# Turning the probabilities as float32r, one block later, after a move inside SBUF: a perceiver block on one core

## The chip, the core and the metric

The kernel runs on one core of one Trainium2 chip. The metric is device time in microseconds (us) of one execution; lower is better. A core has TensorE (PE in the profile, with its weight loads as PEld), VectorE (DVE), ScalarE (ACT), GpSimd (POOL), and SyncE (SP), which here only issues DMAs.

## What is computed

64 tokens `x` of width 512 attend to a context of 6272 rows, then pass a quantised linear block and a second one with a Fourier update. Nearly all the time is the first part, cut here to what matters:

```python
q = (layernorm(x) @ Wq + bq).reshape(64, 8, 4, 128)     # 8 key heads, 4 query heads each
k, v = split(ctx @ Wkv + bkv)                           # 6272 x 8 x 128 each
attn = softmax(einsum(q, k) / sqrt(128))                # per head: 256 query rows x 6272 keys
x = x + einsum(attn, v) @ Wo + bo
x = x + attention_block(layernorm(x), NF4[codes] * scales, lora_a, lora_b)
x = x + base_and_fourier_update(layernorm(x))
```

The 4-bit codes of the second part are expanded to float32 weights, a tile of 128 x 512 at a time.

## The kernel before, in words

The context is walked in 7 chunks of 896 rows (`NCH`, 7 tiles of 128), and in each chunk over the 8 key heads (`NKV`). One head of one chunk is a *block*: 56 blocks, i = 0 to 55 (`NB`). A float32 product is made of three float32r products of rounded parts (`split_matmuls`, L71 to 75): hi x hi, lo x hi, hi x lo. ScalarE rounds a result from PSUM to its hi part, VectorE subtracts to get the lo part.

TensorE's order in block i is written out by hand (`block_work`, L836): the scores of the block (12 products of 448 columns, two halves of the keys for two halves of the 256 query rows), the previous block's weighed values (`prev_values`, 21 products of 256 columns), in even blocks the values of *two* heads for all 7 tiles (`values`, 84 products of 256 columns, into the two banks of `p_kv` in turn), the first half of the next block's keys (`project_keys`, 12 products of 448 columns), then the turns of this block's probabilities in four groups (`turn_probs`, L678 to 691: 4, 4, 4 and 2 transposes of 128 x 128 float32, `probs` as weights, `ident` moving), with the turn of the previous output (`turn_output`) and the second half of the keys between them. Long blocks (even) and short ones (odd) so alternate.

VectorE takes the scores out of PSUM with their minimum (L1314), makes the change of the row maximum (`drop`), splits turned tiles (`pt_lo`, L1291), values (L1279) and keys (L1281), adds the output (`acc`, L1302), and between them merges the lines of one weight tile (L1326, L1330). ScalarE makes the exponentials in place in `probs` (L1171), rounds (L1092, L1103) and draws four of a tile's eight lines (L1127). GpSimd draws the other four (L534), casts codes (L530), joins and scales the tile (L554, L563), and splits context pieces (L522). SP's queue is in order: an issue that waits holds all behind it. It brings the codes (`codes_of`), the scales, the context pieces (`load_ctx`, through one buffer `ctx_st`), and writes each expanded tile to memory (`tile_out`, L400). In the first chunk it also brings the query weights (`load_wq`) and key and value weights (`load_wkv`), and TensorE makes the eight query products (L700) between the other work. In the last chunk freed space takes the weights of what follows, and in the last block the attention output is projected between the last turns (L775).

The two lines that the change centres on:

```python
pe.wait_ge(exp_ready, 2 * i + 2)
m = nc.tensor.transpose(p_t[:, c % 2, col:col + P], probs[:, r, t * P:(t + 1) * P], ident[:])
```

Of the kernel before, what the change touches and what calls it, by code (L numbers as in the profile page):

```python
# [17 lines left out]
P = 128  # L18
# [47 lines left out]
PAIR_PIECES = (5, 5, 5, 1)  # L66
# [62 lines left out]
def whole(nc, ctx_t, x, wq, bq, wkv, bk, bv, codes, scales, weights, wo, bo, lora_a, lora_a_down, lora_b, lora_b_down,  # L129
# [4 lines left out]
    with ExitStack() as st:  # L134
# [8 lines left out]
        pt_hi = sb(st, "pt_hi", [P, CT, ROWS], F32R)  # L143
        pt_lo = sb(st, "pt_lo", [P, CT, ROWS], F32R)
# [8 lines left out]
        slots = sb(st, "slots", [P, 7, TW], F32)  # L153
# [18 lines left out]
        pool_passed = sem("pool_passed")  # L172

        NB = NCH * NKV
        KV_USES = CT + 4

        ACT_LINES = ((1, 1), (2, 2), (4, 4), (5, 5))

        def v_use(s, h, t):
            return 2 + KV_USES * (4 * s + h // 2) + t

        def k_use(s, h, c):

            return 2 + KV_USES * (4 * s + h // 2) + CT + 2 * (h % 2) + c

        def v_bank(h, t):
            return (h // 2 + t) % 2

        def k_bank(h, c):
            return (h // 2 + 1 + c) % 2
# [116 lines left out]

        def tile_of(n, j):  # L310
            return tile_quarters(n)[:, 2 * j:2 * j + 2]
# [53 lines left out]
        def _(sp):  # L365
# [35 lines left out]

            def ring_slots(h):

                first, end = AHEAD[h]
                freed = (end - 1 - RING_ODD) // 4
                if freed < 0:
                    sp.wait_ge(kv_psum, k_use(NCH - 2, NKV - 2, 1) + 1)
                else:
                    sp.wait_ge(kv_psum, k_use(NCH - 1, 2 * freed, 1) + 1)
                for n in range(first, end):  # L410
                    load_slot(n)
# [26 lines left out]
            def chunk(s, last):  # L438
                piece = 0
                for pair in range(NKV // 2):  # L440
# [3 lines left out]
                    def load(q):  # L444
                        if not last and q < PAIR_PIECES[pair]:
                            load_ctx(s + 1, piece + q, start and q == 0)
# [4 lines left out]
                    load(0)  # L451
                    codes_of(n + 2)
                    if start:
                        load_wq(4)
                    load(1)
                    if start:
                        load_wq(5)
                        load_wkv(4)
                        load_wkv(5)
                    tile_out(n)  # L460
                    scales_of(n + 1)
                    if start:
                        load_wq(6)
# [5 lines left out]
                    if start:  # L469
                        load_wq(7)  # L470
                    load(2)
                    load(3)
                    if not end:
                        codes_of(n + 3)
                    if start:
                        load_wkv(6)
                        load_wkv(7)
# [18 lines left out]
                    piece += PAIR_PIECES[pair]  # L496
# [19 lines left out]
        def _(pool):  # L516
# [20 lines left out]
            def first_lines(n, first=False):  # L537
# [4 lines left out]
                line(6, 6)  # L542
# [49 lines left out]
            for dst, src in ((bq_sb, bq), (bk_sb, bk), (bv_sb, bv)):  # L592
                pool.dma_start(dst[:], src).then_inc(vecs_in, 16)
            narrow(0, True)
            first_lines(0, True)

            def chunk(s, par, last):
                piece = 0
                for pair in range(NKV // 2):
                    n = NKV * s + 2 * pair  # L600

                    def split(q):
                        if not last and q < PAIR_PIECES[pair]:
                            split_ctx(s + 1, piece + q, 1 - par)

                    if s == 0 and pair == 1:
# [6 lines left out]
                    last_line(n)  # L613
                    narrow(n + 1)
                    split(0)
                    add_rowsum(n, 2 * pair)
                    join(n)
                    first_lines(n + 1)
                    split(1)
                    split(2)  # L620
                    last_line(n + 1)
# [3 lines left out]
                    if end:  # L625
                        wait_apart(pool, kv_psum, k_use(NCH - 1, NKV - 2, 1) + 1, pool_passed)
# [6 lines left out]
                    join(n + 1)  # L633
                    first_lines(n + 2)
                    split(4)
                    piece += PAIR_PIECES[pair]

# [8 lines left out]
            last_line(NB)  # L646
# [7 lines left out]
            last_line(NB + 1)  # L654
# [3 lines left out]
        def _(pe):  # L658
            def project_keys(bank, half, h, c, k):
# [3 lines left out]
                m = split_matmuls(nc, p_kv[:, bank, 0:HALF], wkv_hi[:, k, cols], wkv_lo[:, k, cols],  # L663
# [5 lines left out]
            def static_first(i):  # L669
                return isinstance(i, int) and i == 0  # L670

            def turn_output(i):

                pe.wait_ge(o_out, i + 1)
                if not static_first(i):
                    pe.wait_ge(ot_added, i)
# [4 lines left out]
            def turn_probs(i, c, skip):  # L681

                if c == 0:
                    pe.wait_ge(exp_ready, 2 * i + 2)
                if not skip:
                    pe.wait_ge(pt_split, 4 * i + c - 1)
                for t in range(2 * c, min(2 * c + 2, CT)):
                    for r in range(RT):
                        col = (t % 2) * ROWS + r * P
                        m = nc.tensor.transpose(p_t[:, c % 2, col:col + P], probs[:, r, t * P:(t + 1) * P], ident[:])  # L690
                m.then_inc(pt_psum, 1)

            def query_product(h):

                pe.wait_ge(wq_in[h % 2], 16 * (h // 2 + 1))
                if h >= 1:
                    pe.wait_ge(q_out, h)
                for k in range(KT):
                    for i in range(2):
                        m = nc.tensor.matmul(p_o[HALVES[i], 0:TW // 2], xt[:, k], wq_sb[h % 2][:, k, HALF_COLS[i]],  # L700
# [12 lines left out]
            def scores(i, h, kuse, static):  # L713
                if i < NKV:
                    pe.wait_ge(q_split, h + 1)
                for c in range(2):
                    pe.wait_ge(kv_split, kuse + c + 1)
                    for r in range(RT):
                        bank = p_s[:, r, 0:HALF] if c == 0 else p_kv[:, k_bank((h - 1) % NKV, r), 0:HALF]
                        if c == 0 and not static:  # L720
                            pe.wait_ge(scores_out, 4 * i - 3 + r)
                        m = split_matmuls(nc, bank, q_hi[:, h, r * P:(r + 1) * P],
# [4 lines left out]
            def values(s, h, half, queries={}):  # L727
                if s == 0:
                    pe.wait_ge(wkv_split, wkv_turn(h + 1) + 1)
                for t in range(CT):  # L730
                    for work, head in queries.get(t, ()):
                        work(head)
                    if t < 2:
                        pe.wait_ge(scores_out, 4 * (NKV * s + h) + 4)
                    pe.wait_ge(kv_split, v_use(s, h, t) - 1)
                    cols = slice((NKV + h) * D, (NKV + h + 2) * D)
                    for k in range(KT):
                        keys = slice(t * P, (t + 1) * P)
                        m = split_matmuls(nc, p_kv[:, v_bank(h, t), 0:2 * D], ctx_hi[half][:, k, keys],
                                          ctx_lo[half][:, k, keys], wkv_hi[:, k, cols], wkv_lo[:, k, cols],  # L740
                                          start=(k == 0), stop=(k == KT - 1))
                    m.then_inc(kv_psum, 1)

            def prev_values(s, h):

                i = NKV * s + h - 1
                hp = (h - 1) % NKV
                pair = 4 * s + h // 2 - (1 if h % 2 == 0 else 0)
                pe.wait_ge(pt_split, 4 * i + 4)
                pe.wait_ge(kv_split, 2 + KV_USES * pair + CT)  # L750
# [978 lines left out]
```

## Time and profile before

| | us |
|---|---|
| median of 3 runs | 1031.01 |
| lowest, highest | 1030.47, 1032.99 |
| span of the profiled execution, first to last instruction | 1028.8 |

The profiled execution is one more execution, and its own time beside its span isn't listed apart from the three runs. Busy times are shares of the span. TensorE's records overlap, as a product is started before the last has drained, so the pace is read from start to start and not from a record's length.

### The profile page before, as it was taken

The numbers are of one execution on the slowest core, as the hardware profiler recorded it, in microseconds if no ns is written. First come the engines' busy times: TensorE is split into PE (matmuls) and PEld (weight loads), VectorE is DVE, ScalarE is ACT, GpSimd is POOL, SyncE is SP. The second block draws the span as 40 slices with busy tenths as digits, with TensorE's granted clock in tenths as the row PEclk, the third lists the DMA queues.
The fourth block names the chain that finished last, engine by engine and source line by source line (L and its number), as shares of the span: only waits on it lengthen the run. The fifth ranks groups of instructions, "written<-read, shape, count | busy, mean of one in ns | idle before, by whom it ended". The sixth has DMA issues, their size and how long they took to land.

```text
span 1028.8 us, 19701 instructions
## 1 busy us (share of the span) xinstructions
PE 1015.2 (99%) x7083; PEld 934.4 (91%) x7083; DVE 752.1 (73%) x1680; ACT 590.3 (57%) x1254; POOL 482.4 (47%) x640
## 2 busy tenths in 40 slices
PE   8999999999999999999999999999999999999998
PEld 6889999999999999999999999999999999999744
DVE  5777778766877677767776687767776687767766
ACT  6456666555665567555665566555665566565431
POOL 2344554455444555445544555545545534544341
PEclk9999999999999999999999999999999999999999
DMA  9832211122212222122211222221222213552895
GB/s 321 263 107 59 65 56 58 58 70 76 60 51 65 65 60 70 42 70 70 70 58 50 71 61 65 64 57 59 68 55 68 72 42 122 168 153 84 250 351 175
DMA packets 74097, 99.01 MB, mean 96 GB/s; under 512 B 8752, under 2 KB 43072, under 8 KB 74000
## 3 DMA queue, kind: packets, MB, share of 16 engines
q1 hardware_dynamic: 72384, 95.95, 30.9%
q10 hardware_dynamic: 1424, 1.51, 0.4%
q8 instruction: 57, 0.93, 0.4%
q0 software_dynamic: 192, 0.29, 0.1%
q14 instruction: 40, 0.33, 0.1%
HBM read 82.91 MB, written 14.81 MB: 95 GB/s over the span
## 4 chain that ended last, share of the span: by engine, by line
PE 93%; DVE 4%; ACT 1%; DMA 1%; issue 1%; ACTq 0%; POOL 0%; DVEq 0%; POOLq 0%
PE p_kv L73 20%; PE p_kv L74 20%; PE p_kv L75 20%; PE p_t L690 8%; PE p_o L73 4%; PE p_o L74 4%; PE p_o L75 4%; PE p_s L73 2%; PE p_s L74 2%; PE p_s L75 2%; PE p_s L775 2%; PE p_o L700 1%; PE p_ot L678 1%; DVE slots L1326 1%; DVE probs L1314 1%; DMA ctx_st<-in_ctx_t 1%
## 5 line engine op out<-in xcount | busy, mean ns | idle before, releaser
L534 POOL TENSOR_SCALAR slots<-code 128x512 f32<-128x512 bf16 x232 | 154.4, 665 | 223.3 <-DVE slots L1330 150.3
L1326 DVE TENSOR_TENSOR slots<-slots 128x512 f32<-128x512 f32 x232 | 167.7, 723 | 1.9
L1279 DVE TENSOR_TENSOR v_lo<-p_kv,v_hi 128x256 fp32r<-128x256 f32 x196 | 83.2, 424 | 113.2 <-ACT v_hi L1092 113.2
L1127 ACT ACTIVATE slots<-code,drop_and_offsets 128x512 f32<-128x512 bf16 x232 | 148.5, 715 | 28.4 <-POOL slots L554 24.9
L554 POOL TENSOR_TENSOR slots<-slots 128x512 f32<-128x512 f32 x58 | 74.8, 1290 | 185.8 <-DVE slots L1326 185.8
L1092 ACT ACTIVATE v_hi<-p_kv 128x256 fp32r<-128x256 f32 x196 | 75.2, 384 | 146.5 <-PE p_kv L75 146.1
L1281 DVE SCALAR_TENSOR_TENSOR k_lo<-p_kv,bk_sb,k_hi 128x448 fp32r<-128x448 f32 x112 | 76.3, 682 | 104.1 <-ACT k_hi L1092 103.3
L1291 DVE TENSOR_TENSOR pt_lo<-p_t,pt_hi 128x512 fp32r<-128x512 f32 x224 | 133.5, 617 | 23.7 <-ACT pt_hi L1103 23.6
L1092 ACT ACTIVATE k_hi<-p_kv,bk_sb 128x448 fp32r<-128x448 f32 x112 | 70.8, 633 | 132.0 <-PE p_kv L75 131.0
L1103 ACT ACTIVATE pt_hi<-p_t 128x512 fp32r<-128x512 f32 x224 | 114.9, 541 | 40.4 <-PE p_t L690 40.4
L73 PE MATMUL p_kv<-wkv_hi,ctx_even_hi 128*128 128x256 f32 x448 | 126.4, 282 | 0.2 <-issue 0.2
L75 PE MATMUL p_kv<-wkv_hi,ctx_even_lo 128*128 128x256 f32 x448 | 125.9, 281 | 0.0
L74 PE MATMUL p_kv<-wkv_lo,ctx_even_hi 128*128 128x256 f32 x448 | 125.8, 281 | 0.0
L1171 ACT ACTIVATE probs<-probs,mins 128x896 f32<-128x896 f32 x112 | 115.5, 1033 | 0.0
L690 PE MATMUL p_t<-ident,probs 128*128 128x128 f32 x784 | 113.1, 272 | 0.2 <-ACT probs L1171 0.2
L73 PE MATMUL p_o<-pt_hi,v_hi 128*128 128x256 f32 x392 | 111.0, 283 | 0.0
L74 PE MATMUL p_o<-pt_lo,v_hi 128*128 128x256 f32 x392 | 110.9, 283 | 0.0
L75 PE MATMUL p_o<-pt_hi,v_lo 128*128 128x256 f32 x392 | 110.8, 283 | 0.0
L690 PEld LDWEIGHTS p_t<-ident,probs 128*128 128x128 f32 x784 | 95.4, 140 | 15.0 <-issue 0.8
L73 PE MATMUL p_kv<-ctx_even_hi,wkv_hi 128*128 128x448 f32 x256 | 99.2, 388 | 0.6 <-issue 0.5
L74 PE MATMUL p_kv<-wkv_lo,ctx_odd_hi 128*128 128x256 f32 x336 | 95.1, 283 | 0.0
L75 PE MATMUL p_kv<-wkv_hi,ctx_odd_lo 128*128 128x256 f32 x336 | 94.9, 282 | 0.0
(239 smaller groups left out, 2705.0 us busy)
## 6 DMA issues: line engine op xcount, KB each, us to landing
code<-in_codes SPq DMA_DIRECT2D x58, 256.0 KB, 2.7
scale<-in_scales SPq DMA_DIRECT2D x114, 128.0 KB, 3.1
expanded_weights<-slots SPq DMA_DIRECT2D x56, 256.0 KB, 2.1
ctx_st<-in_ctx_t SPq DMA_DIRECT2D x96, 112.0 KB, 2.0
ring_hi<-expanded_weights SPq DMA_DIRECT2D x22, 256.0 KB, 6.0
ring_lo<-expanded_weights SPq DMA_DIRECT2D x22, 256.0 KB, 6.1
wq_hi<-in_wq SPq DMA_DIRECT2D x4, 1024.0 KB, 7.5
wq_lo<-in_wq SPq DMA_DIRECT2D x4, 1024.0 KB, 7.3
```

Of the source, the lines that this page charges most:

```text
L73: nc.tensor.matmul(out, hi, rhi, start=start, stop=False)
L74: nc.tensor.matmul(out, hi, rlo, start=False, stop=False)
L75: return nc.tensor.matmul(out, lo, rhi, start=False, stop=stop)
L534: nc.gpsimd.tensor_scalar(slots[:, slot, :], code16[:], LINES[j][0], LINES[j][1], ALU.mult, ALU.add).then_inc(pool_lines, 1)
L690: m = nc.tensor.transpose(p_t[:, c % 2, col:col + P], probs[:, r, t * P:(t + 1) * P], ident[:])
L1092: nc.scalar.activation(dst, src, ACT.Identity, bias=0.0 if bias is None else bias).then_inc(kv_rounded, 1)
L1103: nc.scalar.activation(pt_hi[:, 2 * c:2 * c + n, :].rearrange("p t q -> p (t q)"), p_t[:, c % 2, 0:n * ROWS], ACT.Copy).then_inc(pt_rounde ...
L1127: nc.scalar.activation(slots[:, slot, :], code16[:], ACT.Identity, bias=offsets[:, k:k + 1], scale=LINES[j][0]).then_inc(act_lines, 1)
L1171: nc.scalar.activation(probs[:, r, :], probs[:, r, :], ACT.Exp, bias=mins[:, h, r, now:now + 1], scale=-1.0, accum_out=rowsum[:, par, r:r ...
L1279: nc.vector.tensor_tensor(dst, src, hi.bitcast(F32), ALU.subtract).then_inc(kv_split, 1)
L1291: nc.vector.tensor_tensor(pt_lo[:, 2 * c:2 * c + n, :].rearrange("p t q -> p (t q)"), p_t[:, c % 2, 0:n * ROWS], pt_hi[:, 2 * c:2 * c + n, ...
L1326: nc.vector.tensor_tensor(slots[:, slot, :], slots[:, slot, :], slots[:, other, :], ALU.max).then_inc(merged, 1)
```

## The change

- `turn_probs` for block i - 1 now stands in block i, behind that block's scores. SP first copies the two halves of `probs` inside SBUF into a second tile `probs_r`, bit for bit, and the turn reads that as float32r with an identity of float32r. The last block alone (i = 55) is still turned in float32 from `probs`.
- VectorE waits for the copy before it writes the next scores; SP waits for the earlier turns (`pt_psum`) and each half's exponentials.
- The values of two heads are made over two blocks: 4 tiles in the even one, 3 in the odd one. The first and the last pair make all 7 in the even one.
- The turned tiles have a ring of 4 places instead of 7, and the weighing is done in two parts (tiles 0 to 3, tiles 4 to 6). The space pays for `probs_r`, as does one line slot less.
- The first half of the next keys goes to `p_s` instead of `p_kv`, the orders of ScalarE, VectorE and GpSimd follow, with GpSimd's line 6 drawn only after the second merge, into a slot that this has freed. Context pieces are spread anew (5 a pair of blocks).

Cut to its core:

```diff
+        PT_TILES = 4
+        probs_r = sb(st, "probs_r", [P, RT, CHUNK], F32R)
+        ident_r = sb(st, "ident_r", [P, P], F32R)
-        ACT_LINES = ((1, 1), (2, 2), (4, 4), (5, 5))
+        ACT_LINES = ((2, 2), (5, 5), (1, 1), (4, 4))
+        SPLIT_TILE = 4
+        def value_tiles(i):
+            if i in (0, NB - 2):
+                return range(CT)
+            if i in (1, NB - 1):
+                return range(0)
+            return range(SPLIT_TILE) if i % 2 == 0 else range(SPLIT_TILE, CT)
+        def k_place(h, c):
+            return p_s[:, 0, 0:HALF] if c == 0 else p_kv[:, h % 2, 0:HALF]
...
+            def move_probs(i):
+                if i > 0:
+                    sp.wait_ge(pt_psum, 4 * i)
+                for r in range(RT):
+                    sp.wait_ge(exp_ready, 2 * i + 1 + r)
+                    sp.dma_start(probs_r[:, r].bitcast(F32), probs[:, r]).then_inc(probs_moved, 16)
...
                     load(0)
+                    move_probs(n)
                     codes_of(n + 2)
                     load(1)
+                    load(2)
                     tile_out(n)
                     scales_of(n + 1)
+                    load(3)
...
+                        move_probs(n + 1)
                         codes_of(n + 3)
...
-            def last_line(n):
-                wait_apart(pool, merged, 6 * n + 1, pool_passed)
+            def last_lines(n):
+                wait_apart(pool, merged, 6 * n + 2, pool_passed)
                 line(7, 1)
+                line(6, 3)
...
-                if c == 0:
-                    pe.wait_ge(exp_ready, 2 * i + 2)
+                if i < NB - 1:
+                    pe.wait_ge(probs_moved, 32 * (i + 1))
+                        if i < NB - 1:
+                            m = nc.tensor.transpose(p_t[:, c % 2, col:col + P].bitcast(F32R), probs_r[:, r, keys], ident_r[:])
...
+            def block_work(s, h, half):
+                scores(i, h)
+                turn_probs(i - 1, 0)
+                turn_probs(i - 1, 1)
+                next_keys(i, h, half, 0)
+                weigh_values(i - 1, 0, SPLIT_TILE)
+                turn_probs(i - 1, 2)
+                turn_probs(i - 1, 3)
+                if i > 2:
+                    turn_output(i - 2)
+                for t in value_tiles(i)[:SPLIT_TILE]:
+                    value_tile(i, h, half, t)
+                next_keys(i, h, half, 1)
+                weigh_values(i - 1, SPLIT_TILE, CT)
...
+            (ScalarE)
+                output_out(i - 2); round_probs(i - 1, 0); round_probs(i - 1, 1)
+                weigh(i, h, half, 0); weigh(i, h, half, 1)
+                round_keys(i, h, 0)
+                round_probs(i - 1, 2); round_probs(i - 1, 3)
+                (value tiles, with lines and a context piece between); round_keys(i, h, 1)
...
+            (VectorE)
+                if i > 0:
+                    dve.wait_ge(probs_moved, 32 * i)
+                score_stats(i, h, half)
+                split_probs(i - 1, 0); split_probs(i - 1, 1)
+                merge(i, 0); merge(i, 1)
+                split_keys(i, h, 0)
+                merge(i, 2)
+                split_probs(i - 1, 2); split_probs(i - 1, 3)
+                add_output(i - 2, (h - 2) % NKV)
+                (three times: split_values, merge); split_keys(i, h, 1)
```

The lines for ScalarE and VectorE are gathered from their `block_work`, several to a line.

## Rows read from the trace of the kernel before

**Rows 1.** The page's head: busy us (share of the span) and instructions of each engine.
```profile
PE 1015.2 (99%) x7083; PEld 934.4 (91%) x7083; DVE 752.1 (73%) x1680; ACT 590.3 (57%) x1254; POOL 482.4 (47%) x640
```

**Rows 2.** The chain that ended last, shares of the span by engine and by line.
```profile
PE 93%; DVE 4%; ACT 1%; DMA 1%; issue 1%; ACTq 0%; POOL 0%; DVEq 0%; POOLq 0%
PE p_kv L73 20%; PE p_kv L74 20%; PE p_kv L75 20%; PE p_t L690 8%; PE p_o L73 4%; PE p_o L74 4%; PE p_o L75 4%; PE p_s L73 2%; PE p_s L74 2%; PE p_s L75 2%; PE p_s L775 2%; PE p_o L700 1%; PE p_ot L678 1%; DVE slots L1326 1%; DVE probs L1314 1%; DMA ctx_st<-in_ctx_t 1%
```

**Rows 3.** Stretches: length, each engine's busy us (instructions), clock, DMA share, GB/s.
```profile
0.00:48.00 48.00, 43.46 (x276) 34.16 (x277) 29.17 (x65) 24.42 (x45) 13.34 (x28) 1.00 0.89 292
48.00:157.40 109.40, 106.99 (x739) 99.06 (x738) 81.76 (x182) 66.15 (x140) 54.73 (x70) 1.00 0.27 82
157.40:922.30 764.90, 764.88 (x5291) 730.66 (x5290) 566.70 (x1268) 457.33 (x982) 378.72 (x498) 1.00 0.24 69
```

**Rows 4.** The chain in order of time: start, us, what (pieces on one line merged).
```profile
156.69 0.66 PE p_t L690 x6
...
519.10 0.44 PE p_t L690 x4
...
921.62 0.66 PE p_t L690 x6
```

**Rows 5.** Timeline of TensorE: start, us of the record, instruction.
```profile
506.39 0.28 PE L73 MATMUL p_kv<-wkv_hi,ctx_odd_hi 128*128 128x256 f32 x1
...
516.47 0.36 PE L73 MATMUL p_kv<-ctx_odd_hi,wkv_hi 128*128 128x448 f32 x1
...
518.93 0.60 PE L690 MATMUL p_t<-ident,probs 128*128 128x128 f32 x4
```

**Rows 6.** Groups on TensorE with shapes apart: count | busy us, mean ns | idle before.
```profile
L690 PE MATMUL p_t<-ident,probs 128*128 128x128 f32 x784 | 113.1, 272 | 0.2 <-ACT probs L1171 0.2
...
L700 PE MATMUL p_o<-wq_hi,xt 128*64 128x256 f32 x64 | 7.8, 385 | 0.0
```

**Rows 7.** Weight loads (PEld), groups with shapes apart, as rows 6.
```profile
L690 PEld LDWEIGHTS p_t<-ident,probs 128*128 128x128 f32 x784 | 95.4, 140 | 15.0 <-issue 0.8 <-ACT probs L1171 0.7 <-DVE pt_lo L1291 0.4
L74 PEld LDWEIGHTS p_kv<-wkv_lo,ctx_even_hi 128*128 128x128 f32 x448 | 84.4, 188 | 0.0
...
L700 PEld LDWEIGHTS p_o<-wq_hi,xt 128*64 128x64 f32 x64 | 4.2, 136 | 2.5 <-issue 0.6
```

**Rows 8.** DMA issues: count, KB each, median us to landing.
```profile
wq_hi<-in_wq SPq DMA_DIRECT2D x4, 1024.0 KB, 7.5
...
ctx_raw<-in_ctx_t SPq DMA_DIRECT2D x2, 448.0 KB, 5.9
```

**Rows 9.** What SP's queue waited for: us in total, times, longest.
```profile
SPq L400 <- POOL slots L563: 351.6, 55, 7.7
```

**Rows 10.** The chain in the first chunk: start, us, what.
```profile
48.79 5.40 DMA ctx_st<-in_ctx_t
54.70 2.06 ACT probs L1171 x4
...
90.43 0.93 DVE pt_lo L1291 x2
91.36 2.18 DVE probs L1314 x8
93.97 0.59 DVE acc L1302 x2
94.57 0.60 DVE slots L1330
...
95.81 0.98 DVE slots L1326
```

**Rows 11.** Groups on ScalarE and VectorE, as rows 6.
```profile
L1092 ACT ACTIVATE v_hi<-p_kv 128x256 fp32r<-128x256 f32 x196 | 75.2, 384 | 146.5 <-PE p_kv L75 146.1
L1092 ACT ACTIVATE k_hi<-p_kv,bk_sb 128x448 fp32r<-128x448 f32 x112 | 70.8, 633 | 132.0 <-PE p_kv L75 131.0
...
L1279 DVE TENSOR_TENSOR v_lo<-p_kv,v_hi 128x256 fp32r<-128x256 f32 x196 | 83.2, 424 | 113.2 <-ACT v_hi L1092 113.2
```

More of the change, by code:

```diff
@@ L65, with ctx_piece @@
 PIECES = KT * (CHUNK // PIECE)
-PAIR_PIECES = (5, 5, 5, 1)
+PT_TILES = 4
+PLACES = 5
+FIRST_WQ_PIECE = 5
+def ctx_piece(s, pair, place):
+    if s > 0:
+        piece = PLACES * pair + place
+    elif pair < 2:
+        piece = ((0, 1, PIECES, 2, 3), (4, PIECES, 5, 6, 7))[pair][place]
+    else:
+        piece = PLACES * pair + place - 2
+    return piece if piece < PIECES and s < NCH - 1 else None
 EPS = 1e-5
@@ L442, in chunk, with load @@
                     start = n == 0
-                    def load(q):
-                        if not last and q < PAIR_PIECES[pair]:
-                            load_ctx(s + 1, piece + q, start and q == 0)
+                    def load(place):
+                        piece = ctx_piece(s, pair, place)
+                        if piece is not None:
+                            load_ctx(s + 1, piece, start and piece == 0)
                     end = last and pair == NKV // 2 - 1
@@ L541, in first_lines @@
                 line(0, 0)
-                line(6, 6)
                 if not first:
@@ L597, in chunk, with split @@
             def chunk(s, par, last):
-                piece = 0
                 for pair in range(NKV // 2):
                     n = NKV * s + 2 * pair
[L602 to L606, printed above, removed]
+                    def split(place):
+                        piece = ctx_piece(s, pair, place)
+                        if piece is not None:
+                            split_ctx(s + 1, piece, 1 - par)
+                    if s == 0 and pair == 2:
                         wait_apart(pool, q_split, NKV, pool_passed)
@@ L633, in chunk @@
                     join(n + 1)
+                    split(4)
                     first_lines(n + 2)
-                    split(4)
-                    piece += PAIR_PIECES[pair]
             chunk(0, 0, False)
@@ L725, in scores @@
                         m.then_inc(scores_psum, 1)
[L727 to L742, printed above, removed]
@@ new lines, in weigh_values @@
+            def weigh_values(i, first, last):
+                if first == 0 and i > 0:
+                    pe.wait_ge(o_out, i)
+                pe.wait_ge(pt_split, 4 * i + (2 if last <= PT_TILES else 4))
+                pe.wait_ge(kv_split, kv_number["v", i // 2, last - 1] + 1)
+                d = slice((i % 2) * D, (i % 2 + 1) * D)
+                for t in range(first, last):
+                    m = split_matmuls(nc, p_o[:, 0:ROWS], v_hi[:, t, d], v_lo[:, t, d], pt_hi[:, t % PT_TILES],
+                                      pt_lo[:, t % PT_TILES], start=(t == 0), stop=(t == CT - 1))
+                if last == CT:
+                    m.then_inc(o_psum, 1)
@@ L1205, in block_work @@
                     round_probs(i, c)
[L1206 to L1212 removed]
+                divide(NKV - 2)
                 for c in range(2, 4):
                     round_probs(i, c)
[L1215 to L1218 removed]
@@ L1219, in block_work @@
-                round_ctx(s, h, half, 2 if h % 2 == 0 else 4, last)
-                if last and h >= 2:
-                    divide(h - 2)
-                lines(i + 1)
             act.dma_start(wkv_piece(wkv_raw, 0), wkv_piece(wkv, 0)).then_inc(wkv_in[0], 16)
```

651 lines of the change are left out of this document (363 added, 288 removed).

## The prediction

> **What bounds the kernel now.** I read the page's busy rows first: TensorE is busy in 99% of the 1028.8 us span, VectorE in 73% [rows 1]. Busy alone proves little, since matmuls overlap, so I went to the chain that ended last: 93% of it is TensorE, and the turns of the probabilities (L690) are 8% of the span by themselves [rows 2]. In the stretch from 157 to 922 us, at a granted clock of 1.00 (the 2.4 GHz level), TensorE has 764.88 of 764.90 us filled, while VectorE has 567, ScalarE 457 and GpSimd 379 [rows 3]. Between the two points 156.69 and 921.62 of the chain lie 23 pairs of blocks: 33.26 us a pair [rows 4].
>
> Is a pair made of work alone, or are waits hidden in it? The timeline gives the pace, start to start. 84 value products of 256 columns go from 506.39 to 516.47: 0.120 us each. 12 key products of 448 columns go from 516.47 to 518.93: 0.205 us [rows 5]. Turns of 128 columns take 0.66 us for 6, or 0.44 for 4: 0.110 us each [rows 4]. A pair has 72 products at 0.205 (14.76), 84 + 42 at 0.120 (15.12), 28 + 4 turns at 0.110 (3.52): 33.40 us. That is the measured 33.26 within half a per cent. So nothing waits in the steady state; only work taken off TensorE shortens it, and new waits lengthen it.
>
> **The change part by part.**
> *The turn as float32r.* 55 blocks x 14 = 770 turns go from float32 to float32r; the 14 of the last block stay, and so do the output's. No row shows a float32r product of 128 columns. Three rows bound it. Nearest below: the line through the two float32r paces, (0.205 - 0.120)/192 = 0.00044 us a column, gives 0.063 us at 128. Half of today's pace, 0.055, is the low end. The high end is today's 0.110 or worse: an ordinary float32 product leaves two records (the query products on `wq_hi`: 64 records for 4 heads x 4 x 2 = 32 products [rows 6]), and a turn that became two records would cost 0.22. I take 0.063, for two reasons. Today's turn lasts 272 ns, near the 280 of 256 float32r columns though it has half as many, so its columns are slow ones [rows 5, 6]. And its weight load is not the limit: it takes 140 ns, where an ordinary load takes 136 for 64 columns and 188 for 128 [rows 7]; the turn's load of 128 columns is as short as one of 64. Gain: 770 x 0.047 = 36.2 us. Low end 0.055: 42.4. With 0.22: a loss of 85 us.
>
> The Trainium skill, "TensorE: Matmul & The Clock Gate", section LDWEIGHTS, speaks against this: a load takes its columns divided by 1.2 in ns, and the section after it keeps the faster load for types other than FP32. By that rule 128 columns pace a turn at 0.107 us, and the sum would be 2 us instead of 36. The trace agrees for the float32r loads (188 against 136 ns for twice the columns) and disagrees for today's turns, whose load is 48 ns shorter.
>
> *The move.* Each block adds two DMAs of 448 KB inside SBUF on SP's queue: 110 in all, 49 MB on top of 99. DMA is at 0.24 in the steady stretch [rows 3], so bandwidth is there; what counts is landing. I time a block from its first score product at the forecast paces: scores end at 2.46, eight turns at 2.96, the first half of the next keys at 5.42, four weighed tiles at 6.86, six turns at 7.24, the output's turn at 7.46. SP may issue the move once those six turns are through and the exponentials done: 7.4. VectorE overwrites the probabilities after the first scores of the next block, 16.1 in a short block (15.3 + 0.6 + the 0.16 by which a product's record of 0.36 outlasts its pace [rows 5]). So the two moves together have 8.7 us. No move inside SBUF is in the trace; 1024 KB from memory land in 7.5 us, 448 KB in 5.9, both in the crowded start [rows 8]. I take 7.5 for the pair, being the row of nearest size: hidden, 1.2 us to spare. What stands behind the move on SP: the codes, a piece of the context, the weight tile out. SP waits 352 us for GpSimd at the tile out alone today [rows 9], so two more issues a block lie inside its waiting. A late move would hold SP, TensorE's turns and VectorE's score output at once.
>
> *Turning one block later.* TensorE's work is the same; the exponentials get a whole block. What is late next is VectorE's order: scores out, two splits of turned tiles, merges, keys, two splits, output, first value tile. In the back-to-back stretch from 90 us, four score outputs take 2.18, the reduction 0.43 (91.36 + 2.18 to 93.97), two tile splits 0.93 (0.60 + 0.33), the output 0.59, a merge 0.60 [rows 10]; a key split of 448 columns I take like a tile split of 512. From the last score at 2.62: 3.60 scores done, 4.80 two splits (the weighing wants them at 5.42), 6.0 two merges. The key split waits for ScalarE: 3.60 + 0.1 to start + 2.06 exponentials + 0.63 rounding = 6.4 [rows 10, 11]; it ends at 7.0, a merge at 7.6, the next splits (rounded at 7.9, 0.6 after their turns) at 8.8, the output at 9.4, the first value tile (its product ends at 8.90 + 0.16, rounding 0.38, split 0.42 [rows 11]) at 9.86. The third value tile, 1.44 us after the second begins, needs that bank at 10.34. So 0.5 us are spare. I take no stall; the other end is rival B.
>
> *V over two blocks, four turned tiles, other orders of lines, context pieces and GpSimd.* A long and a short block of together 33.26 become two of 16.8 and 15.3; the number of instructions is unchanged. VectorE's 567 us and GpSimd's 379 fit into some 735. GpSimd's later line waits for two merges (6.0 in a block) and is wanted by the fifth, after two value tiles (10.3): cost 0, covered by TensorE's stream; without that cover it is B's stall.
>
> *Start and end.* From 48 to 157 us TensorE is idle for 2.4 of 109.4 us [rows 3], and part of the chain there is VectorE's [rows 10]: with even blocks this may go. Against it, the first move stands on SP behind up to 2 MB of weights; the chain has a landing of 5.40 us of that kind at 48.79 [rows 10]. Between -2.4 and +5.4 I take 0: no row says which is nearer. In the last block one block's turns move past the last scores, with output projections between as before: 0.
>
> *Sum:* 1028.8 - 36.2 = 992.6 us of span; 2.2 lie between this span and the median 1031.0 (the profiled execution has no time of its own in the list, and the runs lie from 1030.5 to 1033.0). 992.6 + 2.2 = 995.
>
> **The rivals.**
> *A: the turn keeps its pace.* If a float32r turn loads as float32r products do (188 ns, 104 of it for columns by the slope (188 - 136)/64 = 0.81 ns), it goes at 0.104 to 0.110: a gain of 0 to 4.6, and with the start's -2.4 to +5.4, time 1024 to 1036, middle 1030. For: all float32r loads in the trace are long ones. Against: the turns' loads are short though their data are as wide. (It is what the rule of the Trainium skill above would do here.)
> *B: VectorE's chain eats the gain.* Merges in the same stretch took as much as 0.98 instead of 0.60 [rows 10]; three such ahead of the first value tile add 1.1, 0.6 past what is spare: 55 x 0.6 = 33 us, time 1028; one such, 0: 995. For: half a microsecond is little in a chain of 7. Against: GpSimd is mostly waiting for just these merges.
> *C: the moves land late, slower than before.* It decides from 8.7 us after issue and passes break-even at 8.7 + 36.2/55 = 9.4. If the second lands only after the first, 5.9 each [rows 8], 11.8: 3.1 us a block, 55 x 3.1 = 170, time 1165. Against: that row is of the start, where DMA is 0.89 busy [rows 3], not 0.24.
> *D: the turn becomes dearer*, two records at 0.22: 1031 + 85 = 1116. No row speaks for it but the ordinary float32 product.
>
> **How the numbers follow.** Forecast 0.60 (985 to 1003: 1031 - 42.4 - 2.4 = 986 at the low end, less 1 for rounding; 995 + 5.4 and 2 of B's at the high), A 0.19, B partly or wholly 0.08, C 0.09, D 0.04. A measurement of this kernel tells 0.3% (3 us) from no change. Faster: 0.60, 0.06 of A and 0.05 of B: 0.71. Same: 0.10 of A and 0.02 of B: 0.12. Slower: C and D 0.13, 0.03 of A, 0.01 of B: 0.17. The range has to reach into A to hold 8 in 10: 985 to 1033.
>
> **What would show it.** Right: six turns in 0.38 us, a pair in about 31.9, TensorE still full from 160 us on, no wait of L690's successor on a DMA. A shows as turns at 0.110 and loads of 188 ns; B as first value splits later than 10.3 us into a block and value products waiting for VectorE; C as turns or score outputs waiting for the move; D as twice the turn records. I am wrong if turns are fast and the pair is not: then the cover that I reckoned was missing.

## The result and the profile after

| | us |
|---|---|
| before, median of 4 runs | 1031.55 |
| after, median of 4 runs | 1018.95 (1017.25 to 1021.18) |
| ratio, 95% interval | 0.988 (0.9861 to 0.9898) |
| span of the profiled execution after | 1015.7 (1028.8 before) |

The kernel is 12.6 us faster. That lies inside the range of 985 to 1033, but it is a third of the 36 us that the forecast of 995 wanted, and it lies between the forecast's own range (up to 1003) and rival A's (from 1024).

The page of after, its head and its chain, stands against [rows 1] and [rows 2]:

```profile
PE 996.8 (98%) x7083; PEld 922.3 (91%) x7083; DVE 744.5 (73%) x1680; ACT 587.4 (58%) x1254; POOL 441.6 (43%) x641
...
PE 91%; DVE 4%; DMA 2%; ACT 1%; issue 1%; SPq 1%; POOL 0%; DVEq 0%; POOLq 0%; ACTq 0%
...
probs_r<-probs SPq DMA_DIRECT2D x110, 448.0 KB, 3.7
```

TensorE still bounds the kernel. The new moves land in 3.7 us (median). DMA and SP's queue have grown in the chain, from 1 to 3% together; we come to that with the start.

The stretches of after (columns as in [rows 3]):

```profile
48.00:157.40 109.40, 103.36 (x711) 95.95 (x710) 83.20 (x187) 67.82 (x142) 53.15 (x72) 0.98 0.43 143
157.40:922.30 764.90, 764.71 (x5406) 735.16 (x5405) 573.30 (x1300) 465.98 (x1008) 349.81 (x508) 1.00 0.38 128
```

Two things are to be seen. From 157 us on TensorE has no gaps, as before: no new wait has appeared there. Between 48 and 157 us it idles 6.0 us (109.40 - 103.36) instead of 2.4, at a granted clock of 0.98 instead of 1.00.

The chain in order of time gives the steady pace (start, us, what):

```profile
156.55 0.64 PE p_t L769 x8
161.10 0.47 PE p_t L769 x6
...
904.89 0.64 PE p_t L769 x8
```

23 pairs of blocks take 748.34 us: 32.54 us a pair. It was 33.26 [rows 4], and 31.9 was forecast. So the steady part gains 0.72 us a pair, some 20 us in 27.5 pairs, and the rest of the kernel loses some 7.

Now the turn itself, first by its groups (columns as in [rows 6, 7]):

```profile
L769 PE MATMUL p_t<-ident_r,probs_r 128*128 128x128 f32 x770 | 79.3, 244 | 0.0
...
L769 PEld LDWEIGHTS p_t<-ident_r,probs_r 128*128 128x128 f32 x770 | 76.3, 141 | 4.3
```

There is one record a turn, and a load's record is as short as before, 141 against 140 ns. The records say little about the pace. The weight loads' own timeline says more: in a full stream a load starts just when the product ahead of it starts, so a product's start is read from the start of the *next* load (the ordinary product recorded at 514.86 has the last load below at 514.86). Start, us, instruction:

```profile
513.95 0.65 PEld L769 LDWEIGHTS p_t<-ident_r,probs_r 128*128 128x128 f32 x7
514.55 0.19 PEld L88 LDWEIGHTS p_s<-ctx_odd_hi,wkv_hi 128*128 128x128 f32 x1
514.65 0.19 PEld L89 LDWEIGHTS p_s<-ctx_odd_lo,wkv_hi 128*128 128x128 f32 x1
514.86 0.19 PEld L90 LDWEIGHTS p_s<-ctx_odd_hi,wkv_lo 128*128 128x128 f32 x1
```

The first of the seven loads belongs to the second of the eight turns, so the first turn starts at 513.95. Seven steps to 514.55 are 0.086 us each. The step in which an ordinary load follows is longer, 0.10 to 0.11 (514.55 to 514.65; the median of such steps between 160 and 880 us is 0.108). Then the ordinary product takes its usual 0.21. Eight turns so take 0.70 us; eight at [rows 4]'s 0.110 take 0.88, and the forecast wanted 0.50. (The chain's piece of 0.64 us is too short, and the piece of the product behind it too long, 0.27 instead of 0.21: it puts the border at a modelled start.)

### The profile page after: what moved, and what is told of

It is laid out like the page before. It is cut to its first block, busy times and chain, and to the rows that moved or that the text cites. A ratio compares the mean times of both kernels' runs of the same rounds, so it can differ in the third digit from the quotient of the medians.

```text
span 1015.7 us, 20355 instructions
## 1 busy us (share of the span) xinstructions
PE 996.8 (98%) x7083; PEld 922.3 (91%) x7083; DVE 744.5 (73%) x1680; ACT 587.4 (58%) x1254; POOL 441.6 (43%) x641
## 4 chain that ended last, share of the span: by engine, by line
PE 91%; DVE 4%; DMA 2%; ACT 1%; issue 1%; SPq 1%; POOL 0%; DVEq 0%; POOLq 0%; ACTq 0%
PE p_kv L88 16%; PE p_kv L90 16%; PE p_kv L89 15%; PE p_s L88 7%; PE p_s L90 6%; PE p_s L89 6%; PE p_t L769 6%; PE p_o L88 4%; PE p_o L90 4%; PE p_o L89 4%; PE p_s L849 1%; PE p_ot L753 1%; DMA wkv_raw<-in_wkv 1%; DMA ctx_st<-in_ctx_t 1%; PE p_o L783 1%
## 5 line engine op out<-in xcount | busy, mean ns | idle before, releaser
L610 POOL TENSOR_SCALAR slots<-code 128x512 f32<-128x512 bf16 x232 | 147.8, 637 | 247.3 <-DVE slots L1466 164.2
L1210 ACT ACTIVATE pt_hi<-p_t 128x512 fp32r<-128x512 f32 x224 | 110.0, 543 | 117.0 <-PE p_t L769 111.4
L1239 ACT ACTIVATE slots<-code,drop_and_offsets 128x512 f32<-128x512 bf16 x232 | 158.6, 713 | 6.5 <-POOL code L606 3.4
L630 POOL TENSOR_TENSOR slots<-slots 128x512 f32<-128x512 f32 x58 | 77.7, 1339 | 165.5 <-DVE slots L1466 165.5
L1430 DVE TENSOR_TENSOR pt_lo<-p_t,pt_hi 128x512 fp32r<-128x512 f32 x224 | 128.7, 614 | 11.0 <-ACT pt_hi L1210 10.0
L1417 DVE SCALAR_TENSOR_TENSOR k_lo<-p_kv,bk_sb,k_hi 128x448 fp32r<-128x448 f32 x56 | 38.3, 684 | 105.7 <-ACT k_hi L1198 105.7
L88 PE MATMUL p_kv<-wkv_hi,ctx_odd_hi 128*128 128x256 f32 x336 | 96.9, 288 | 0.0
L1198 ACT ACTIVATE k_hi<-p_kv,bk_sb 128x448 fp32r<-128x448 f32 x56 | 35.6, 636 | 91.6 <-PE p_kv L90 91.6
L88 PEld LDWEIGHTS p_kv<-wkv_hi,ctx_even_hi 128*128 128x128 f32 x448 | 84.5, 189 | 1.1 <-issue 1.1
L89 PEld LDWEIGHTS p_kv<-wkv_lo,ctx_even_hi 128*128 128x128 f32 x448 | 84.5, 189 | 0.0
```

Source lines behind the costliest of these rows:

```text
L88: nc.tensor.matmul(out, hi, rhi, start=start, stop=False)
L89: nc.tensor.matmul(out, hi, rlo, start=False, stop=False)
L610: nc.gpsimd.tensor_scalar(slots[:, slot, :], code16[:], LINES[j][0], LINES[j][1], ALU.mult, ALU.add).then_inc(pool_lines, 1)
L630: nc.gpsimd.tensor_tensor(slots[:, 0, :], slots[:, 0, :], slots[:, 4, :], ALU.subtract).then_inc(joined, 1)
L1198: nc.scalar.activation(dst, src, ACT.Identity, bias=0.0 if bias is None else bias).then_inc(kv_rounded, 1)
L1210: nc.scalar.activation(pt_hi[:, at:at + n, :].rearrange("p t q -> p (t q)"), p_t[:, c % 2, 0:n * ROWS], ACT.Copy).then_inc(pt_rounded, 1)
```

## The experiments

Nine kernels were run, in three groups, each beside the kernel before on the same chip; the ratios are to that. The expectations call "theory L" the reading that the weight load paces a float32r turn, and that the product behind a group of turns is long because its own load is not covered. The first half held and the second did not, as will be seen.

**Order and move alone.** The turns of after, made in float32 again:

```diff
-    m = nc.tensor.transpose(p_t[:, c % 2, col:col + P].bitcast(F32R), probs_r[:, r, keys], ident_r[:])
+    m = nc.tensor.transpose(p_t[:, c % 2, col:col + P], probs_r[:, r, keys].bitcast(F32), ident[:])
```

> The kernel after the change with its turns back in float32 (read from the moved tile, with the old identity): the move, the new order, the ring of four and the rest stay. Theory L (a float32r turn is paced by its weight load, about 0.08 us, and too short to cover the longer load of the ordinary product behind it): turns back at 0.110 us, first ordinary product behind eight turns back from 0.27 to 0.21 us; 1019.0 + 770 x 0.030 + 55 x 0.085 = 1046.8 us. Rival M (the moves' traffic is what makes that first product long): it stays at 0.27, time 1042. Rival O (order and move cost nothing, as the prediction had it): 1031.5, and then the pace of the turns alone explains the gain.

Measured: 1035.39 us, ratio 1.0041 (1.0026 to 1.0056). The sum of theory L in the expectation has a sign wrong: if the product behind gets back to 0.21, its 4.7 us come off and are not added, 1019.0 + 23.1 - 4.7 = 1037.4. The run lies 2 below that. Its loads:

```profile
507.07 0.79 PEld L769 LDWEIGHTS p_t<-ident,probs_r 128*128 128x128 f32 x7
507.83 0.19 PEld L88 LDWEIGHTS p_s<-ctx_odd_hi,wkv_hi 128*128 128x128 f32 x1
507.94 0.19 PEld L89 LDWEIGHTS p_s<-ctx_odd_lo,wkv_hi 128*128 128x128 f32 x1
```

Turns step by 0.109 us, the last step is 0.11. The chain gives a pair, again over 23:

```profile
160.10 0.87 PE p_t L769 x8
...
922.26 0.87 PE p_t L769 x8
```

That is 33.14 us a pair. What follows: the type of the turn alone is worth 0.60 us a pair and 16.4 us in all (1035.4 against 1019.0), not 36.2. And the rest of the change costs 4 us by itself, though its steady pair is 0.12 us *shorter* than before's 33.26: the loss is outside the steady part. Rival M (the moves' traffic makes the product behind long) is out: the moves are here, and the excess is gone. Rival O is out as well, by the 4 us.

**The turns alone, in the old order.** In the kernel before, with no move; the turns of blocks 0 to 54 read constant data (the rounded queries):

```diff
-    m = nc.tensor.transpose(p_t[:, c % 2, col:col + P], probs[:, r, t * P:(t + 1) * P], ident[:])
+    if i < NB - 1:
+        m = nc.tensor.transpose(p_t[:, c % 2, col:col + P].bitcast(F32R), q_hi[:, 0, r * P:(r + 1) * P], ident_r[:])
+    else:
+        m = nc.tensor.transpose(p_t[:, c % 2, col:col + P], probs[:, r, t * P:(t + 1) * P], ident[:])
```

> The kernel before with float32r turns in the old places, and no move: the turns of blocks 0 to 54 read a constant float32r tile (the rounded queries) in place of the probabilities, so that the weights of the values are wrong numbers while the amount of work is the same; the identity comes by GpSimd's queue. Theory L: turns at 0.080, and two ordinary products a block stand right behind turns (+0.065 each) and one output turn (+0.02): 1031.5 - 23.1 + 55 x 0.15 = 1016.7 us. Rival M (the products' excess, and the turns' pace over 0.063, come from the moves' traffic): 995 to 1008. Rival A of the prediction (no float32r turn is faster) is out already; it would be 1031.

Measured: 1016.58 us, ratio 0.986 (0.9845 to 0.9875): theory L's figure. The old order has no room for the move, so this isn't a kernel to use, but it gives the price of the turns without the move and the new order: 14.4 us. Its chain gives a pair, again over 23:

```profile
156.98 0.47 PE p_t L693 x6
...
907.87 0.47 PE p_t L693 x6
```

That is 32.65 us a pair, 0.61 less than before and as much as the 0.60 of the exchange above; over 27.5 pairs it is 16.8. Some 2.4 of these are lost ahead of the steady part: the first piece stands at 156.98, no earlier than before's 156.69 [rows 4], though the turns ahead of it are faster too (why wasn't tried; this edit also brings the identity by another queue). Both ways of taking the type alone, 14.4 here and 16.4 above, are under half of the forecast.

**No move.**

```diff
                 if i > 0:
-                    sp.wait_ge(pt_psum, 4 * i)
+                    return
...
-                if i < NB - 1:
-                    pe.wait_ge(probs_moved, 32 * (i + 1))
+                if i == 0:
+                    pe.wait_ge(probs_moved, 32)
...
-                if i > 0:
-                    dve.wait_ge(probs_moved, 32 * i)
+                if i == 1:
+                    dve.wait_ge(probs_moved, 32)
```

> The kernel after the change with the move of block 0 alone; the turns of blocks 1 to 54 read those same moved probabilities again, behind the exponentials of their own block, so the later probabilities are left out of the result. Theory L (moves are hidden and cost TensorE nothing): the same as after within 3 us, 1016 to 1021, turns at 0.080. Rival M: without 108 moves of 448 KB the turns go at 0.063 or the product behind them at 0.21: 1001 to 1014. If SP's issues or waits for the move delay the first chunk: -1 to -5 us, all before 160 us.

Measured: 1020.04 us, ratio 0.9889 (0.9874 to 0.9904), the same as after. In its steady stretch the DMA share is 0.23 instead of 0.38, and nothing else moves:

```profile
157.40:922.30 764.90, 764.68 (x5405) 735.17 (x5405) 576.03 (x1298) 464.92 (x1006) 351.43 (x508) 1.00 0.23 72
```

So 108 moves of 448 KB cost nothing in time. Nor do they cause the loss at the start: without them (block 0's move stays) TensorE idles 7.5 us between 48 and 157 us.

**Half a load.** Only 64 of a turn's 128 columns of weights; as many columns move as before:

```diff
+    if 0 < i < NB - 1:
+        half = slice(keys.start, keys.start + 64)
+        m = nc.tensor.transpose(p_t[0:64, c % 2, col:col + P].bitcast(F32R), probs_r[:, r, half], ident_r[:])
```

> The kernel after the change with half of each turn left out from block 1 to 54: 64 of 128 columns of weights are loaded and turned, the same 128 columns move. Theory L (the load paces a turn): pace from 0.080 to the moving columns' own, 0.060 to 0.065, 756 x 0.017 = 13 us less: 1006 us. Rival P (0.080 is the product's own pace, whatever is loaded): 0.080 stays, 1019 us. The product behind the turns keeps its 0.27 under L, for its own load is as long as before.

Measured: 1006.79 us, ratio 0.9764 (0.9746 to 0.9782), against 1006 expected of theory L and 1019 of rival P. Its loads, and then its group:

```profile
509.72 0.47 PEld L770 LDWEIGHTS p_t<-ident_r,probs_r 128*64 128x64 f32 x7
510.14 0.19 PEld L88 LDWEIGHTS p_s<-ctx_odd_hi,wkv_hi 128*128 128x128 f32 x1
510.25 0.19 PEld L89 LDWEIGHTS p_s<-ctx_odd_lo,wkv_hi 128*128 128x128 f32 x1
...
L770 PEld LDWEIGHTS p_t<-ident_r,probs_r 128*64 128x64 f32 x756 | 55.9, 110 | 5.7
```

Seven steps in 0.42 us: 0.060 each. The edit also halves the rows that a turn writes to PSUM, but after itself has a step as short with whole turns. It is there where the load of the output's float32 turn (L753) stands behind six turns:

```profile
518.93 0.14 PEld L753 LDWEIGHTS p_ot<-ident,o_t 128*128 128x128 f32 x1
...
518.99 0.14 PEld L753 LDWEIGHTS p_ot<-ident,o_t 128*128 128x128 f32 x1
...
519.10 0.19 PEld L88 LDWEIGHTS p_kv<-wkv_hi,ctx_odd_hi 128*128 128x128 f32 x1
```

The sixth turn starts at 518.93, and the output's first turn at 518.99. So one and the same turn takes 0.06 us ahead of this float32 load, 0.086 ahead of a load of its own kind and 0.10 to 0.11 ahead of an ordinary one. This settles the pace: the next product's load sets it. The 128 columns that move need 0.060 us or less, so the forecast's 0.063 was right for them. In the kernel after they wait for the 128 columns of weights, which need 0.086. The float32 load fits into the 0.06, though its record is as long.

**The same turn as an ordinary product.**

```diff
-    m = nc.tensor.transpose(p_t[:, c % 2, col:col + P].bitcast(F32R), probs_r[:, r, keys], ident_r[:])
+    m = nc.tensor.matmul(p_t[:, c % 2, col:col + P], probs_r[:, r, keys], ident_r[:], start=True, stop=True)
```

> The kernel after the change with each float32r turn as an ordinary float32r product with the identity, not in the transpose mode (the probabilities lose what float32r cannot hold). Theory L (an ordinary float32r load of 128 columns is the long one, 188 ns, and paces): 0.105 us a turn, 770 x 0.025 = 19.3 us more, less the 4.7 of the products behind, which are covered then: 1033.6 us. Rival W (the load's pace goes by its columns and type alone, whatever the mode): 0.080, 1019 us. The forecast's own line through the paces of float32r products: 0.063, 1006 us.

Measured: 1035.22 us, ratio 1.0036 (1.0023 to 1.0049).

```profile
506.67 0.86 PEld L769 LDWEIGHTS p_t<-ident_r,probs_r 128*128 128x128 f32 x7
507.45 0.19 PEld L88 LDWEIGHTS p_s<-ctx_odd_hi,wkv_hi 128*128 128x128 f32 x1
507.56 0.19 PEld L89 LDWEIGHTS p_s<-ctx_odd_lo,wkv_hi 128*128 128x128 f32 x1
```

Same data, same columns, same type; only the mode differs, and the load steps by 0.111 us instead of 0.086. Rival W is out, and so is the forecast's line for this case. This is what rival A foresaw, and what the Trainium skill, "TensorE: Matmul & The Clock Gate", section LDWEIGHTS, states (columns divided by 1.2, an estimate of 0.107 us for 128): the trace agrees for an ordinary product and disagrees for a transpose. Here no load behind the turns is longer than theirs, and the product behind them starts one such step, 0.11 us, after the last turn.

**The last turn of eight in float32.** Theory L's second half put to the test:

```diff
+    if i < NB - 1 and c == 1 and t == 3 and r == 1:
+        m = nc.tensor.transpose(p_t[:, c % 2, col:col + P], probs_r[:, r, keys].bitcast(F32), ident[:])
```

> The kernel after the change with the eighth turn of each block, the one ahead of an ordinary product, back in float32 (read from the moved tile). Theory L (the ordinary load needs a turn of 0.110 us to hide behind): that turn +0.03, the product behind it from 0.27 to 0.21: 55 x 0.035 = 1.9 us less, 1017 us. Rival (the change of type from float32r with short loads to float32r with long ones costs something by itself): 0.27 stays, 1019.0 + 55 x 0.03 = 1020.6 us.

Measured: 1017.08 us (1014.25 to 1021.67), ratio 0.9858 (0.9834 to 0.9881): the interval holds both the expected figure and no change. The loads decide:

```profile
516.52 0.78 PEld L771 LDWEIGHTS p_t<-ident_r,probs_r 128*128 128x128 f32 x7
517.24 0.14 PEld L769 LDWEIGHTS p_t<-ident,probs_r 128*128 128x128 f32 x1
517.28 0.22 PEld L88 LDWEIGHTS p_s<-ctx_odd_hi,wkv_hi 128*128 128x128 f32 x1
517.41 0.19 PEld L89 LDWEIGHTS p_s<-ctx_odd_lo,wkv_hi 128*128 128x128 f32 x1
```

The second of these loads, and with it the first turn, starts at 516.72 (one by one the loads stand at 516.52, 516.72, 516.81); from there to the ordinary product's start at 517.41 are 0.69 us, against 0.70 in after. So hardly anything is won. An ordinary load does hold the turn ahead of it, at 0.10 to 0.11 instead of 0.086, but a float32 turn takes its 0.11 anyway. The rest of the excess of 0.065 us was the turns' own time, told under the next product's name. This half of the theory falls.

**The start: two issues exchanged.** SP's queue in the first chunk of before, and of after (start, us, instruction):

```profile
41.22 0.34 SPq L400 DMA_DIRECT2D expanded_weights<-slots  x1
...
43.34 0.60 SPq L417 DMA_DIRECT2D wq_hi<-in_wq  x1
45.54 0.56 SPq L417 DMA_DIRECT2D wq_lo<-in_wq  x1
48.79 7.51 SPq L371 DMA_DIRECT2D ctx_st<-in_ctx_t  x2
```

```profile
49.43 0.33 SPq L463 DMA_DIRECT2D expanded_weights<-slots  x1
...
50.99 0.60 SPq L484 DMA_DIRECT2D wq_hi<-in_wq  x1
51.63 0.63 SPq L484 DMA_DIRECT2D wq_lo<-in_wq  x1
52.31 0.62 SPq L434 DMA_DIRECT2D ctx_st<-in_ctx_t  x1
```

In after the first expanded tile goes out 8.2 us later: the chain has GpSimd's last step on it, the scaling, at `48.12 1.29 POOL slots L639` right ahead of SP's issue. Why it is late stands in the rows of VectorE and GpSimd, first of before and then of after (in brackets the idle time before, and what ended it):

```profile
37.59 0.68 DVE L1326 TENSOR_TENSOR slots<-slots 128x512 f32<-128x512 f32 x1
...
38.45 1.27 POOL L554 TENSOR_TENSOR slots<-slots 128x512 f32<-128x512 f32 x1 [5.29 <-DVE slots L1326]
```

```profile
37.61 0.68 DVE L1466 TENSOR_TENSOR slots<-slots 128x512 f32<-128x512 f32 x1
...
46.02 0.67 POOL L598 TENSOR_TENSOR ctx_odd_lo<-ctx_st,ctx_odd_hi 128x224 fp32r<-128x224 f32 x1 [12.80 <-ACT ctx_odd_hi L1228]
46.65 1.29 POOL L630 TENSOR_TENSOR slots<-slots 128x512 f32<-128x512 f32 x1
```

VectorE ends the tile's last merge at 38.3 us in both. In before GpSimd joins the lines (L554) right behind it. In after GpSimd idles 12.80 us for ScalarE's rounding of a context piece, splits that piece (L598), and only then joins (L630): with the pieces spread anew, the split of the second piece, which stood behind the join, stands ahead of it.

Meanwhile SP holds two query weights and a context piece behind it. The piece is then in the chain with `52.31 10.10 DMA ctx_st<-in_ctx_t`, where [rows 10] have 5.40. In the first trial the piece goes ahead of the weights:

```diff
+                        load(3)
                         load_wq(6)
                         load_wq(7)
-                        load(3)
```

> The kernel after the change with one SP issue moved: the third context piece goes ahead of the last two query weights instead of behind them. Theory S (part of the start's loss is that this piece shares the DMA engines with 2 MB issued just ahead of it): the piece lands in some 5.4 us instead of 10.1, TensorE idles 2 to 3 us instead of 6.0 between 48 and 157 us: 1019.0 - 4 = 1015 us. Rival T (the loss is in what stands before it: SP is held at the first tile's way out until 49.4 us, where it was 41.2 in the kernel before): 1018 to 1019, for piece and weights stay as late as they are.

Measured: 1019.73 us, ratio 0.9887 (0.9873 to 0.99): rival T, no gain. TensorE now idles 7.6 us (109.4 - 101.81) between 48 and 157 us: it waits 1.3 for the weights and 5.2 for a query product.

**The start: three issues ahead of the tile.**

```diff
                         move_probs(n)
-                        tile_out(n)
-                        scales_of(n + 1)
                         load_wq(6)
                         load_wq(7)
                         load(3)
+                        tile_out(n)
+                        scales_of(n + 1)
```

> The kernel after the change with the last two query weights and the third context piece issued ahead of the first tile's way out instead of behind it. Theory T (SP's queue is held at that tile until 49.4 us, 8.2 later than before, and all behind it is late by as much): the whole loss of the start returns, 1019.0 - 4.7 = 1014 us, TensorE idle 48 to 157 us back to 2 to 3 us. Rival S: no better than the exchange of two issues alone, since it is the 2 MB that slow the piece. If neither: 1019.

Measured: 1015.18 us, ratio 0.9835 (0.9822 to 0.9849), against 0.988 for after: 4.6 us less, as theory T had it. Windows of 2 us show what the late piece did in after, and then what is there with the early loads (columns as in [rows 3]):

```profile
62.00:64.00 2.00, 1.08 (x6) 0.65 (x4) 0.00 (x0) 1.57 (x4) 0.81 (x2) 1.00 0.42 164
64.00:66.00 2.00, 0.67 (x3) 0.61 (x4) 1.40 (x4) 1.10 (x4) 1.74 (x3) 0.93 0.46 137
66.00:68.00 2.00, 2.00 (x9) 1.72 (x7) 1.32 (x5) 1.61 (x4) 1.92 (x3) 0.50 1.00 329
68.00:70.00 2.00, 2.00 (x14) 1.93 (x13) 1.43 (x6) 1.43 (x4) 0.28 (x1) 0.72 1.04 370
```

```profile
66.00:68.00 2.00, 2.00 (x17) 1.92 (x16) 1.93 (x7) 1.73 (x6) 1.92 (x3) 1.00 0.68 240
...
48.00:157.40 109.40, 105.41 (x730) 98.20 (x729) 85.96 (x191) 70.14 (x146) 56.67 (x74) 1.00 0.42 144
```

In after TensorE was busy 1.75 of the 4 us from 62, with one wait of 2.26, and in the next 2 us the granted clock is 0.50, the level of 1.2 GHz: products of 448 columns go at 0.37 us instead of 0.205. With the early loads it is full and at 1.00 there. Over the whole stretch it idles 4.0 us instead of 6.0 (theory T had 2 to 3). What the clock lacks of 1.00 costs after 0.14, 1.00 and 0.56 us in the three windows from 64 us, 1.7 in all. Together that is 3.7 of the 4.6.

The spans of the two profiled executions, 1015.7 and 1013.4 us, are only 2.3 apart, for with the early loads the clock fell elsewhere:

```profile
0.00:48.00 48.00, 42.53 (x263) 33.15 (x264) 27.64 (x63) 23.23 (x43) 9.20 (x25) 0.96 0.89 286
```

In after it is 1.00 there; 0.04 of 48 us is 1.9. The clock also differs between executions of one kernel: after's took 1017.25 and 1017.49 us at a mean clock of 0.998, 1020.41 and 1021.18 at 0.995. So part of the 4.6 between the medians is the clock's, and how much of that the early loads save for good isn't shown.

**Two of VectorE's orders besides.** On top of the early loads, the query product of block 1 ahead of a merge, and two turned heads ahead of two tile splits in the last block:

```diff
-                merge(i, 0)
                 if i == 1:
                     finish_query(5)
+                merge(i, 0)
...
-                split_probs(i - 1, 0)
-                split_probs(i - 1, 1)
                 attention_t(0)
                 attention_t(1)
+                split_probs(i - 1, 0)
+                split_probs(i - 1, 1)
```

> The kernel with the three early loads, and two of VectorE's orders exchanged as well: in block 1 the query product is taken out of PSUM ahead of the first merge (0.68 us earlier; TensorE waits 2.9 us for it), and in the last block the first two turned heads are written out ahead of the two tile splits (TensorE waits 1.33 us for them, and they would be ready some 0.85 us earlier). If both waits are on the path: 1015.2 - 1.5 = 1013.7 us. Rival: what is behind them is late in its turn (the tile splits are wanted by the weighing 2 us later, the merges by GpSimd), and it is 1015.2 or more.

Measured: 1014.95 us (1012.37 to 1016.16), ratio 0.9843 (0.983 to 0.9857): not to be told from the early loads alone. TensorE's waits for the two:

```profile
PE p_ot L783 <- DVE q_f L1568: 2.9, 1, 2.9
...
PE p_s L849 <- DVE ot L1502: 0.4, 1, 0.4
```

The first didn't move, so the merge was not what made it late. The second fell from 1.3 to 0.4 us, which is under what these runs can tell. The best version is thus the one with the early loads, at 0.9835 of before.

## Why the prediction was wrong

*The turn's pace.* The step that failed is "I take 0.063", and in it the second reason, "its weight load is not the limit". The load's record of 140 ns was compared with those of other loads, and being the shortest for its size it was taken to be free. But the question was how closely such loads can follow one another, and the trace of before couldn't show that, as its float32 turns step by 0.110, a pace that the loads need not limit. They can follow at 0.086 us (0.10 to 0.11 where the next load is an ordinary one). It was also a float32 load that was read: that one fits into 0.06, and the float32r load, with a record as long, doesn't. The extrapolated 0.063 itself was good: with half a load, or ahead of a float32 load, the turn goes at 0.060. By load starts a block's fourteen turns take 1.19 us (0.70, and 0.49 for the six ahead of the output's turn) instead of 1.53 in the run with float32 turns, as medians of the blocks between 160 and 880 us: 55 x 0.336 = 18.5 us. By the exchange of the type alone it is 16.4; the 2 between the two ways are open. The term was 36.2. The trace had a warning in rival A's row of ordinary loads, and the mechanism of A, pacing by loads, was the right one; its figure, 0.104 to 0.110, is that of another mode. (The Trainium skill, "TensorE: Matmul & The Clock Gate", section Back-to-back issue gap, states about 81 ns for each of a stream of loads and products with 128 moving columns: the trace's 0.086 for the transpose is near it, the 0.111 of the product is not.)

*The move.* Right: hidden. It lands in 3.7 us a DMA where the forecast took 7.5 for the pair, and leaving the moves out changes nothing. Rival C is out.

*VectorE's order.* Right: no stall that counts. From 157 to 922 us TensorE's only wait of record on another engine is this:

```profile
PE p_kv L88 <- DVE v_lo L1415: 0.2, 1, 0.2
```

The reordering even takes 0.12 us off a pair, some 3 us in all, for which the prediction had no term; why wasn't tried. Rival B is out, and D too (one record a turn).

*Start and end.* Taken as 0 between -2.4 and +5.4; the start costs 4.6 us. The prediction named the place, SP's queue with 2 MB of weights, but another delay: not the move that stands ahead of them (the early loads stand behind the same move) but the first tile, which GpSimd joins 8.2 us later. The step that failed here is "cost 0, covered by TensorE's stream", said of "other orders of lines, context pieces and GpSimd": it checked the one line that is drawn later, not the context piece whose split now stands ahead of the join, and "without that cover it is B's stall" looked for the cost on TensorE's side alone. It came out on SP's queue, in the one chunk where loads stand behind a tile. (The rows show GpSimd's wait; no run puts the split back behind the join.) The idle that it made then cost nearly as much again through the clock, 2.0 and 1.7 us in the profiled executions.

The end was taken as 0 as well. From the last block's first score product to the end of the kernel before takes 73.68 us (from 955.16) and after 76.61 (from 939.09), 2.9 more. The 14 turns of block 54, which now stand there, are 1.2 of that. The other 1.7 belong to the new order, for the old order with float32r turns takes 73.8 there; 0.8 of them are a longer wait of TensorE for VectorE's turned heads (1.3 us instead of 0.5).

*The account.* 36.2 forecast, less 19.8 (what the turns fell short by the exchange of the type: 36.2 - 16.4), less 4.6 (start), plus 3.3 (0.12 us in 27.5 pairs): 15.1. Measured are 12.6. Of the 2.5 that are left some 1.7 lie in the last block; no run settles the rest.

## What to carry to other kernels

Here the pace of a turn was the larger of two, its moving columns' and the weight load's of the product behind it, and the faster type helped only the first (0.109 to 0.060 us or less, while the load went from 0.06 or less to 0.086): before a gain is extrapolated from moving columns, look for a row in which loads of that mode follow one another without a gap, and keep the present pace in the range if there is none. Read such paces from the starts of the loads, not from the length of records. And when the order of an engine off the critical path is changed, go through every in-order queue that waits for its results, the first pass of the loop above all: what stands behind such a wait is late by as much.

## What the runs showed of the hardware

- 128 columns of float32r weights load every 0.086 us for a transpose and every 0.111 us for an ordinary product of the same data (records 141 and 191 ns long); 64 columns for a transpose step by 0.060, records of 110 ns. Ahead of a float32 load for a transpose the same whole float32r turn takes 0.06.
- A float32 transpose of 128 columns steps by 0.109 us with a load record of the same 140 ns. So the float32r gain of a turn is 0.023 us, a fifth, where the moving columns alone would have given almost half.
- A recorded start of a product can lie up to 0.07 us ahead of the real one when its load is late: the product behind eight turns is recorded at 514.58, and its next load, which goes with its start, at 514.65.
- A DMA of 448 KB from SBUF to SBUF lands in 3.7 us at a DMA share of 0.38, and 110 of them leave TensorE's paces as they are.
